# A five-layer message-passing kernel on one core: the dense passes of layers 3 and 4 spread over three stages, every second step

## The reference, cut to what matters

```python
# x: 50000 x 128, src, dst: 25000 edges, dst sorted; local = edges only
x = layernorm(x + L0(x, edge_attr, src, dst))      # gated messages, summed by dst
x = layernorm(x + L1(x, src, dst))                 # attention over 25000 edges
h = relu(mean(x[src] by dst) @ W1l.T + b1 + x @ W1r.T)      # L2, first half
y = mean(h[src] by dst) @ W2l.T + b2 + h @ W2r.T            # L2, second half
x = layernorm(x + y)                               # "x3"
h = gat(x, src, dst)                               # L3, edges only
x = layernorm(x + silu(layernorm(h) * g + b) @ out_w + out_b)
```

## Time and profile before

| what | us |
|---|---|
| median of 3 runs (3022.6 to 3034.55) | 3024.89 |
| the profiled execution's own time | 3033.15 |
| its span, first to last instruction | 3031.4 |
| `sage1` with `nodes3`, about 1735 to 2041 | 306 |
| `sage2`, about 2067 to 2314 | 247 |
| `att1` with `nodes4`, about 2337 to 2648 | 311 |
| DVE busy over the span | 2232.0 (74%) |
| ACT busy over the span | 2022.4 (67%) |

### The profile page before, as it was taken

The page is one execution under the profiler, slowest core; times in us unless marked ns, Lnnn a source line. Parts: engine busy times, 40 slices in busy tenths (PEclk is TensorE's granted clock), DMA queues, the critical chain, the costliest instruction groups (busy, mean ns, idle before and its releaser), DMA issues.

```text
span 3031.4 us, 52239 instructions
## 1 busy us (share of the span) xinstructions
PE 1828.3 (60%) x9371; PEld 1361.7 (45%) x9371; DVE 2232.0 (74%) x8475; ACT 2022.4 (67%) x5238; POOL 1897.5 (63%) x1803
## 2 busy tenths in 40 slices
PE   3666666454445543677777676666775666635552
PEld 3565665333333332455555443334664555524442
DVE  6788888766666663787878566665887888888883
ACT  3888888544434342687878688884554888858885
POOL 5777777488888887333333365546775776417775
PEclk9777777667777776788989878887998878855555
DMA  4889898433333333799999799996886988834441
GB/s 145 290 296 300 290 303 295 118 63 62 62 60 60 62 61 57 269 338 337 335 336 343 277 314 329 326 323 196 260 259 206 296 294 289 264 120 159 158 158 50
DMA packets 293490, 663.84 MB, mean 219 GB/s; under 512 B 55198, under 2 KB 88617, under 8 KB 293425
## 3 DMA queue, kind: packets, MB, share of 16 engines
q1 hardware_dynamic: 214609, 549.74, 52.8%
q0 software_dynamic: 78816, 113.45, 16.8%
HBM read 342.83 MB, written 324.08 MB: 220 GB/s over the span
## 4 chain that ended last, share of the span: by engine, by line
DVE 15%; ACT 13%; DMA 11%; issue 9%; PE 8%; DVEq 1%; POOL 1%; SPq 1%; ACTq 0%; POOLq 0%
ACT node_out L1198 8%; DVE n_stats L1520 4%; DMA node_in<-y_nodes 4%; DMA node_in<-x_table 3%; DMA acc_dump<-acc 3%; PE ps L1030 3%; ACT node_x2t L1198 2%; PE ps L1041 2%; DVE acc L1573 1%; DVE node_in L1824 1%; PE ps L1151 1%; DVE node_in L1937 1%; DVE e_stats L1520 1%; PE ps L1023 1%; ACT node_x2t L1299 1%
## 5 line engine op out<-in xcount | busy, mean ns | idle before, releaser
L1198 ACT ACTIVATE node_out<-node_in,n_shift,n_root 128x128 f32<-128x128 f32 (+1 forms) x1176 | 468.2, 482 | 71.2 <-DVE n_shift L1537 70.5
L748 POOL DMA_INDIRECT sums<-gat_sums,dst_safe_i x196 | 185.3, 945 | 301.2 <-DVE pre L1824 240.6
L813 POOL DMA_INDIRECT gat_sums<-sums,add_idx x196 | 321.8, 1642 | 66.7 <-issue 58.2
L1520 DVE BATCH_NORM_STATS2 n_stats<-node_in 128x6 f32<-128x256 f32 (+1 forms) x784 | 279.3, 419 | 79.8 <-DMA node_in<-y_nodes 68.8
L866 POOL DMA_INDIRECT out_dram<-node_x2t,out_index x196 | 212.4, 1084 | 170.5 <-ACT node_x2t L1198 109.7
L756 POOL DMA_INDIRECT src_rows<-x_table,row_i x200 | 201.1, 1005 | 130.9 <-issue 52.2
L756 POOL DMA_INDIRECT sums<-x_table,row_i x192 | 192.6, 1003 | 101.0 <-issue 50.3
L748 POOL DMA_INDIRECT src_rows<-in_x_dram,src_i x196 | 191.1, 975 | 78.5 <-issue 58.8
L748 POOL DMA_INDIRECT own_rows<-x_table,row_i x196 | 191.8, 979 | 65.8 <-issue 53.0
L756 POOL DMA_INDIRECT own_rows<-in_x_dram,dst_safe_i x196 | 192.7, 983 | 59.8 <-issue 57.0
L1207 ACT ACTIVATE t_a<-ps 128x512 f32<-128x512 f32 (+1 forms) x198 | 116.1, 586 | 158.2 <-PE ps L910 158.0
(11 more groups left out here) (358 smaller groups left out, 6571.8 us busy)
## 6 DMA issues: line engine op xcount, KB each, us to landing
x_table<-node_out SPq DMA_DIRECT2D x144, 512.0 KB
own_rows<-x_table SPq DMA_DIRECT2D x245, 256.0 KB, 3.1
node_in<-x_table SPq DMA_DIRECT2D x96, 512.0 KB
acc_dump<-acc SPq DMA_DIRECT2D x147, 264.0 KB
x_table<-new_rows SPq DMA_DIRECT2D x147, 256.0 KB
gat_sums<-node_x2t SPq DMA_DIRECT2D x49, 528.0 KB
node_sums<-gat_sums SPq DMA_DIRECT2D x48, 528.0 KB
node_in<-in_x_dram SPq DMA_DIRECT2D x48, 512.0 KB
```

The source lines that it names most:

```text
L748: g_.indirect_dma_start(out=to[:, g.b, j, 0:width], out_offset=None, in_=tab, in_offset=bass.IndirectOffsetOnAxis(ap=indices(j), axis=0)). ...
L813: g_.indirect_dma_start(out=gat_sums[:, :], out_offset=bass.IndirectOffsetOnAxis(ap=add_idx[:, g.b, j:j + 1], axis=0), in_=sums[:, g.b, j, ...
L1198: last = sc.activation(to[0:pn, g.b, j, :], rows[0:pn, g.b, j, 0:F], ACT.Identity, bias=NORM[k][2][0:pn, g.b, j:j + 1], scale=root[0:pn, j ...
L1520: last = v.bn_stats(NORM[k][0][0:pn, g.b, j:j + 2, :].rearrange("p j c -> p (j c)"), rows[0:pn, g.b, j:j + 2, 0:F].rearrange("p j f -> p f ...
```

## The change

Layers 3's and 4's dense passes are cut in two halves and run every second step of three stages.

- In `sage1`, 25 dense steps of `nodes3` (`early_half`, even steps), and for the same 25 tiles the dense step of layer 4 right behind them (`early4`): DVE adds the constant row to `node_out` in SBUF into `node_y` (`early_x3_more`, lag 3), takes its statistics, ACT normalises into `node_h1` (lag 4), SP stores to the result (lag 5). These 25 tiles are no longer loaded from x3_table.
- In `sage2`, the other 24 dense steps of `nodes3` (`late_half`, even steps).
- In `att1`, the other 24 dense steps of `nodes4` (`late_half`).

A function with a half runs when s - lag is even, as dense step start + (s - lag) / 2. SP's and ACT's loops in these stages become loops of four steps, and DVE's in `att1` too.

```diff
+EARLY_HALF = 25
+LATE_LOOPED = 2 * (DENSE_FULL - EARLY_HALF)
...
-        for lag, stage, count in stages:
-            if 0 <= s - lag < count:
-                stage(step(s - lag))
+        for lag, stage, count, *half in stages:
+            t = s - lag
+            if half and t >= 0 and t % 2 == 0 and t // 2 < count:
+                stage(step(half[0] + t // 2))
+            elif not half and 0 <= t < count:
+                stage(step(t))
...
+def early_half(lag, stage):
+    return (lag, stage, EARLY_HALF, 0)
+def late_half(lag, stage):
+    return (lag, stage, DENSE_STEPS - EARLY_HALF, EARLY_HALF)
...
+            def store_early_out(g):
+                E = flow["early4"]
+                wait_done(sp, E["m_row"], g)
+                sp.dma_start(node_rows(out, 0, g), node_h1[:, g.b, :, :]).then_inc(E["m_out"].sems[g.b], 16)
...   SP, sage1
-            pipeline(sp, DENSE_FULL, edges((0, load_own(L, L["tr_b"], x2_table, own_rows, L["own"])))
-                     + [nodes(0, load_nodes(D, y_nodes, 0, "n_row"))] + edges((1, dump))
-                     + [nodes(2, store_nodes(D, x3_table, SLOTS))] + edges((3, store)))
+            pipeline(sp, STEPS, edges((0, load_own(L, L["tr_b"], x2_table, own_rows, L["own"])))
+                     + [early_half(0, load_y)] + edges((1, dump)) + [early_half(2, store_x3), early_half(5, store_early_out)]
+                     + edges((3, store)), per=4)
...   SP, sage2
-            pipeline(sp, STEPS, edges((0, both), (1, dump), (4, store)))
+            pipeline(sp, LATE_LOOPED, edges((0, both)) + [late_half(0, load_y)] + edges((1, dump)) + [late_half(2, store_x3)]
+                     + edges((4, store)), per=4)
...   ACT, sage1
+            pipeline(act, STEPS, [early_half(1, dense_root), early_half(4, roots(E, "m"))] + edges((2, h1_rows))
+                     + [early_half(1, early_x3), early_half(4, dense_out)] + edges((1, sage_relu), (0, sage_copies)), per=4)
...   ACT, sage2
+            pipeline(act, LATE_LOOPED, [late_half(1, dense_root)] + edges((3, new_x3), (2, root), (0, sage_copies))
+                     + [late_half(1, dense_x3)], per=4)
...   DVE, sage1
+            def early_x3_more(g):
+                wait_done(dve, D["n_row"], g)
+                wait_free(dve, E["m_row"], g)
+                v.tensor_tensor(node_y[:, g.b, :, :], node_out[:, g.b, :, :],
+                                local3_bc[:, None, :].to_broadcast([P, DJ, F]), ALU.add).then_inc(E["m_pre"].sem, 1)
+            pipeline(dve, STEPS, edges((0, plain_sums)) + [early_half(1, dense_shifts), early_half(4, shifts(E, "m"))]
+                     + edges((0, means))
+                     + [early_half(0, dense_moments), early_half(3, early_x3_more), early_half(3, early_x3_moments)], per=4)
...   DVE, sage2
+            pipeline(dve, LATE_LOOPED, edges((3, x3_shifts), (0, sources_landed), run[0], (2, x3_sums), run[1], (2, x3_moments), run[2])
+                     + [late_half(1, dense_shifts)] + edges(run[3], (0, means)) + [late_half(0, dense_moments)], per=4)
...   att1: on SP, ACT and DVE each nodes(...) becomes late_half(...), with per=4
```

More of the change, by code:

```diff
@@ L183, in pipeline @@
 def pipeline(eng, looped, stages, per=2):
[L186 removed]
+    longest = max(lag for lag, *_ in stages)
     def at(s):
[L189 to L191 removed]
+        for lag, stage, count, *half in stages:
[4 more added lines that the diff above has]
+                stage(step(t))
     first = (longest + 3) // 2 * 2 if per == 2 else (longest + 5) // 4 * 4
@@ L198, in pipeline @@
         for h in range(per):
-            for lag, stage, _ in stages:
+            for lag, stage, _, *half in stages:
                 t = first + h - lag
-                stage(Step(i * (per // 2) + t // 2, t % 2, t % 4, i + t // 4))
-    for s in range(first + per * loops, max(lag + count for lag, _, count in stages)):
+                if not half:
+                    stage(Step(i * (per // 2) + t // 2, t % 2, t % 4, i + t // 4))
+                elif t % 2 == 0:
+                    n = half[0] + t // 2
+                    stage(Step(i + n // 2, n % 2))
+    for s in range(first + per * loops, max(lag + count * (2 if half else 1) for lag, _, count, *half in stages)):
         at(s)
@@ L443, in gnn_program @@
                          rings=dict(own=1, stored=1), quads=dict(quad=J)),
-            "nodes4": dict(front=norm("n") + ["n_pre", "n_row"], rings=dict(n_in=1, n_out=1), steps=DENSE_STEPS),
+            "early4": dict(front=norm("m") + ["m_pre", "m_row"], rings=dict(m_out=1), steps=EARLY_HALF),
+            "nodes4": dict(front=norm("n") + ["n_pre", "n_row"], rings=dict(n_in=1, n_out=1), steps=DENSE_STEPS, start=EARLY_HALF),
             "att2": dict(front=["msgd"],
@@ L452, in gnn_program @@
             flow[layer] = {}
-            steps = use.get("steps", STEPS)
+            steps, start = use.get("steps", STEPS), use.get("start", 0)
             for kind, total in (("front", steps), ("back", steps + 1)):
@@ L458, in gnn_program @@
                     per = use.get("per", PER).get(n, 1)
-                    flow[layer][n] = Signal(sems[n], counts[n], per)
-                    counts[n] += per * total
+                    flow[layer][n] = Signal(sems[n], counts[n] - per * start, per)
+                    counts[n] += per * (total - start)
             for n, m in use["rings"].items():
@@ L463, in gnn_program @@
                     sems[n], counts[n] = sem2(n), [0, 0]
-                flow[layer][n] = Ring(sems[n], counts[n], m, steps, n in ("n_in", "n_out", "n_h1", "n_y"))
+                base = [counts[n][b] - 16 * m * ((start + 1 - b) // 2) for b in range(2)]
+                flow[layer][n] = Ring(sems[n], base, m, steps, n in ("n_in", "n_out", "n_h1", "n_y"))
                 counts[n] = flow[layer][n].end
```

39 lines of the change are left out of this document (24 added, 15 removed).

## The result

The changed kernel takes **3048.52 us** (median of 4 runs, 3045.6 to 3053.92) beside 3023.74 us of the kernel before in the same comparison (4 runs, 3020.58 to 3034.55): a ratio of **1.0063, 95% interval 1.0039 to 1.0087**, 25 us slower by the medians. (The ratio is the record's estimate from the single runs of both kernels; it is not the quotient of the two medians, 1.0082, and puts the loss at 19 us. The profiled execution of the change took 3045.6 us, its span is 3043.9 us.

The account below looks back on a forecast made before the run. It took dense traffic piled on the first aggregation and attention to bound the kernel, with no engine full in all three stages. -24 + 6 + 92 - 45 = +29 us, from 3024.89 to 3054 us, slower; range 3005 to 3090.

Parts of the forecast that it names:

- First aggregation, -24: sage1: a step falls from 6.44 to 5.95 us, near ACT's own step; 49 steps save 24 us.
- The end of the stage: +6: End of sage1: two dense normalisations in appended half-empty steps stand before the repair's copies on ACT; +6 us, between 3 and 10.
- Second aggregation, +92: sage2: the dense load, issued behind the wait for pre, stalls DVE 2.1 us every even step; pair 14.0 against 10.16, +92 us.
- +41 predicted for a load in time: sage2, lower bound: the load lands in time and DVE's work alone makes the pair 11.86 us; +41 us.
- Attention, -45: att1: the dense load goes every second step; a pair falls from 12.66 to 10.8 us, saving 45 us.
- the other round: att1: DVE's add and statistics, ACT's rows and query copies, then DVE's products, closing in 10.0 us per pair.
- POOL's term of 10.9: att1: POOL needs 1.07 + 0.29 us a gather, 8 of them 10.9 us a pair.
- Elsewhere, 0: Outside the three stages: longer loop code and added waits for m_out at the last stage cost nothing.
- The load in time: Rival, sage2: the dense load lands in time and DVE alone sets the pair at 11.86; 3003 us, faster; chance 0.14.
- The rival in which the dump decides: sage2: load partly covered, the later dump sets the pair at 12.6 us; sum -4, 3021 us, the same; chance 0.22.
- The gains did not stay small: Rival: sage1 remains at 6.3 us a step, att1 at 11.6 a pair; +66, 3091 us; chance 0.14.

Follow-up runs that it names:

- e1c_load_first: The change, with SP issuing the second aggregation's dense load ahead of the two own-row loads: 3022.55 us, 0.9977 of the kernel before.
- e3_stats_later: The change, with the second aggregation's dense statistics, shifts, ACT's rows and store one step later: 3353.4 us, 0.9944 of the kernel before.
- e5_small_add: The change with the second aggregation's dense load first, and att1's add on one of eight rows for the 24 late tiles: 3341.78 us, one execution.
- c1_change_again: The change unaltered, on another chip where the kernel before took 3369.64 us: 3377.05 us, 1.0009 of the kernel before.
- e8_dump_first: The change, with the second aggregation's dense load and dump both ahead of the own-row loads: 3355.2 us, 1.0024 of the kernel before.

## Why the prediction was right

**First aggregation, -24: right in size.** 5.95 us a step predicted, 5.89 measured. The prediction took it as near ACT's own step; ACT is busy for 246.29 / 280.00 x 5.89 = 5.2 of it (5.4 predicted), and the chain of waits shows a round through ACT and DVE with the new add in it. The load's wait went, the handoff of the shift stayed and grew, as it now stands behind the add. The end of the stage: +6 predicted, 6 found, by the mechanism named.

**Second aggregation, +92: right in its mechanism, 8 us too large.** Each step of the argument is in the rows: SP in lockstep with `pre` (103.1 us of waits), the load 0.67 us behind it (0.69 predicted), the means ending 3.3 behind it (3.14), a landing of 4.34 on average (4.6 taken), a stall of 2.04 (2.1), an even step of 8.62 (8.75) and an odd one of 5.28 (5.3), a pair of 13.90 (14.0). `e1c_load_first` shows the cause: the same load in another place of the same queue, nothing else changed, and the stage loses 33.3 of the 83.6 us. What is left, +50.3, would be the work itself (+41 predicted for a load in time) and the dump; no run separates these two. 24 pairs at 3.74 more are 90 us, the stage is 83.6 longer; the rest must lie in its first and last steps, which were not costed.

**Attention, -45: right in size, 3 us too large, and partly by luck.** POOL was to set the pace at 1.36 us a gather. It takes 1.34, but the chain of waits shows it deciding only up to about 2445. After that the other round decides, which the prediction had put at 10.0 us a pair and which takes 11.1. The step that failed is that term: it was built from DVE's add and statistics with ACT's rows and copies, while the measured round has PE's products and transposes in it (2.08 + 1.71 + 1.72 us from 2513.24 on). The two errors nearly cancel: POOL's term of 10.9 was wrong as the limit and close to the limit's real size.

**Elsewhere, 0: right.** `att2` to the end differs by 0.2 us.

**The rivals.** The load in time does not hold in the change (19 waits for it in 260 us). The rival in which the dump decides does not hold either (3.1 us), but it is what `e1c_load_first` turns into: a pair of 12.48 there, where the rival had said 12.6, and a total 6 us below the kernel before beside it, where the rival had said 4. There the dump goes out ahead of the load and not behind it, so these near numbers do not prove the rival's sum. The page "DMA: Bandwidth & Descriptors" of the Trainium skill (Anatomy of one DMA) would have had 512 KB land in an estimated 3.2 us, by a fit for the gpsimd path; the chain's loads took 3.88 to 5.29, so the measurement decides, and the range over it. The gains did not stay small: 5.89 and 11.0, not 6.3 and 11.6.

**What this says of the change.** Spreading the dense rows frees 63 us in the two crowded stages. It costs 84 in the third, 33 of them only for where one load stands in an in-order queue. With that load moved, the change is worth 0.23% (0.07 to 0.39) against the kernel before. That is the best version found on such a chip; on the others it was `e3_stats_later`, at 0.9944 of the kernel before.

## What to carry to other kernels

When work is moved into a stage that has room on every engine, find the queue that will issue its loads and what that queue is waiting for at that place: a load behind a wait for this step's own result is late by its whole landing time, however idle the DMA engines are. Add up issue, landing and the time until the user asks, from rows of a stage with like traffic; that sum gave the loss here within a tenth. A loss of that kind can be undone by a change of order alone, and the next wait in the queue (here the dump) takes over part of it. A stage that comes out as long as forecast does not show that the named limit was the limit: in the attention part only the chain of waits told that it was not POOL.

## What the runs showed of the hardware that was not expected

**A gather that starts during a DVE instruction with two SBUF inputs ends 0.81 us after it.** POOL's gathers take 0.94 us otherwise; in `att1` of the change (2420 to 2620) 18 of its 18 adds have one beside them that takes over 1.15, and where DVE's instruction began first the gather ends 0.80 to 0.83 us after it. Two rows in order of time:

```profile
2447.89 1.22 DVE L1991 TENSOR_TENSOR node_in<-node_in,local_bc 128x1024 f32<-128x1024 f32 x1
2448.59 1.33 POOL L785 DMA_INDIRECT sums<-x_table,row_i  x1 [0.30 <-issue]
```

The add ends at 2449.11, the gather at 2449.92. In `e5_small_add`, with short adds, none of these is beside a long gather, and the 15 long ones left stand beside `pre`, whose inputs `new_rows` and `gate` both lie in SBUF:

```profile
2768.82 0.69 DVE L1980 TENSOR_TENSOR pre<-new_rows,gate 128x512 f32<-128x512 f32 x1
2768.93 1.40 POOL L785 DMA_INDIRECT sums<-x_table,row_i  x1 [0.30 <-issue]
```

Again 0.82 after it. In `sage2`, where `pre` has one input in PSUM and there is no add, no gather of 2100 to 2300 is over 1.1 us. The add that the change brings into `sage1` does the same to POOL there (7 of 19 adds between 1780 and 2000 have a gather over 1.15 us beside them):

```profile
L785 POOL DMA_INDIRECT src_rows<-x_table,row_i x76 | 76.4, 1005 | 37.8 <-DVE acc L1613 18.9 <-issue 18.8
```

1005 ns, 943 before. The Trainium skill, page "SBUF — State Buffer" (SBUF: two separate sides), says that a DVE operation with two SBUF inputs and a GpSimd operation that reads SBUF exclude each other for the whole instruction, whichever starts first. The trace agrees where DVE started first. Where the gather started first it does not: 30 of the 37 adds in these stretches of `att1` and `sage1` begin inside a running gather, 0.02 to 0.90 us before its end, and all take 1.21 to 1.22 us, as the others do. The measurement decides: the add does not wait for the rest of the gather. In the forecast of `att1` this lengthening was in the 1.07 us that the prediction took from the rows; it had not been known as DVE's doing.

**Chips differ by a tenth on the same program.** The median of the kernel before was 3024 to 3029 us in two groups of runs and 3344 to 3375 in three others, on other chips. The instructions do not take longer there (`t_a` 0.60 us, `pre` 0.69, gathers of `sage2` 946 ns against 943); ACT and DVE stand still again and again, ACT for up to 4.2 us at a time in `c1_change_again` and 6.8 in `e8_dump_first`, ended by nothing that is recorded, and PE waits behind them. One such place of `c1_change_again`:

```profile
2416.43 0.60 ACT L1237 ACTIVATE t_a<-ps 128x512 f32<-128x512 f32 x1 [4.10 <-remote]
...
2417.75 0.60 PE L1128 MATMUL ps<-b_parts,ones_bf 3*128 3x512 bf16 x1 [5.88 <-ACT t_b L1237]
```

There are 8 such waits for `t_a` in 240 us, about one in four steps, which is the length of the looped code. What causes them was not tried and stays open. The ranking of versions depends on the chip: there the later statistics (`e3_stats_later`) were 0.7% better than the load first and the change itself could not be told from the kernel before; on the chip of 3029 us the later statistics, added to the load first, made it 0.7% worse. `e3_stats_later` by itself was not run there.
